# A fused transformer block on one core: unscaled probabilities with inverse sums on the value product, and a front that keeps batch 0 on chip and splits the weights

## What is computed

```python
xn = _layernorm(x, axis=-1)
x = x + attention(xn, w_q, w_kv, w_proj, b_proj) + ffn(xn, ...)

# attention: 16 heads of 32, one key and one value head for all of them, rotary positions
attn = jnp.einsum('bnih,bjh->bnij', q, k)
attn = jnp.where(causal, -jnp.finfo(attn.dtype).max, attn)
attn = jax.nn.softmax(attn, axis=-1)
out = jnp.einsum('bnij,bjd->bind', attn, v)
out = out.reshape(B, S, N_HEADS * HEAD_DIM) @ w_proj.T + b_proj

# ffn: gate logits pick 2 of 4 groups, then 8 of 32 experts for each token;
# every expert works on a latent x @ fc1_w.T of 256; a shared part runs for all tokens
shared = relu2(x @ shared_up_w.T) @ shared_down_w.T
return shared + (sum over picked experts, weighted) @ fc2_w.T
```

## Time and profile before

| | us |
|---|---|
| median of 3 runs | 1771.65 (1771.54 to 1773.84) |
| the profiled execution, span | 1784.5 |
| PE busy | 1640.6 (92%) |
| DVE busy | 1202.6 (67%) |
| ACT busy | 1073.5 (60%) |
| POOL busy | 822.7 (46%) |
| front, about | 100 |
| middle, batch 0, mask to mask | 161.5 |
| middle, each of batches 1 to 6 | 119.1 to 122.0 |

### The profile page before, as it was taken

How to read it: one execution, slowest core, us unless ns; L and a number is a source line. 1 busy time by engine, 2 the same in 40 slices (tenths; PEclk the granted TensorE clock), 3 DMA queues, 4 the chain that set the end, 5 groups by cost and what they waited for, 6 DMA issues and landing times.

```text
span 1784.5 us, 40620 instructions
## 1 busy us (share of the span) xinstructions
PE 1640.6 (92%) x10811; PEld 1385.8 (78%) x10811; DVE 1202.6 (67%) x3666; ACT 1073.5 (60%) x2799; POOL 822.7 (46%) x669
## 2 busy tenths in 40 slices
PE   5836779999999999999999999899999999999999
PEld 5835557777777777777777777689999999999987
DVE  7857876877777867767778678355555555555567
ACT  2324545775675756757757667466666666666652
POOL 0032101442443424434424345177777777777760
PEclk9967889999999999999999999999999999999999
DMA  7983242443434434435434344489999999998894
GB/s 283 372 279 88 55 71 79 137 128 101 157 115 144 126 99 131 135 103 153 137 104 133 102 146 122 135 154 184 186 185 195 194 177 197 210 176 159 139 251 187
DMA packets 193666, 277.91 MB, mean 156 GB/s; under 512 B 37464, under 2 KB 133855, under 8 KB 190884
## 3 DMA queue, kind: packets, MB, share of 16 engines
q0 software_dynamic: 60352, 92.59, 23.9%
q1 hardware_dynamic: 78148, 117.20, 23.0%
q10 hardware_dynamic: 54944, 65.52, 12.5%
HBM read 123.93 MB, written 131.76 MB: 143 GB/s over the span
## 4 chain that ended last, share of the span: by engine, by line
PE 63%; DVE 12%; issue 8%; ACT 4%; DMA 3%; POOL 2%; DVEq 1%; SPq 0%; another core or an unknown queue 0%; ACTq 0%; POOLq 0%
PE e_psH L1644 12%; PE e_psY L1655 11%; PE m_psT L1250 6%; PE m_psU L64 4%; DVE m_sc L1047 4%; PE m_psU L66 4%; PE m_psS L1233 4%; PE m_psU L65 4%; PE m_psO L1274 4%; PE e_psX L1629 3%; PE m_psY L66 3%; PE m_psY L64 3%; PE m_psY L65 3%; POOL sums L1609 2%; ACT m_sc L899 2%
## 5 line engine op out<-in xcount | busy, mean ns | idle before, releaser
L1609 POOL DMA_INDIRECT sums<-e_y,e_where x287 | 445.3, 1551 | 156.5 <-issue 94.4
L823 POOL DMA_INDIRECT slot_rows<-m_row,slots x256 | 268.6, 1049 | 501.1 <-ACT m_sc L899 457.2
L899 ACT ACTIVATE m_sc<-m_sc,m_low 128x512 f32<-128x512 f32 (+3 forms) x512 | 283.7, 557 | 173.9 <-DVE m_low L1047 150.8
L1644 PE MATMUL e_psH<-e_xt,e_w_of 128*128 128x128 f32 x2296 | 303.6, 275 | 3.2 <-ACT e_xt L1504 3.2
L1047 DVE CUSTOM_DVE_ANT_0 m_sc<-m_psS,cst 128x512 f32<-128x512 f32 (+3 forms) x512 | 230.0, 485 | 107.0 <-PE m_psS L1233 104.8
L1655 PE MATMUL e_psY<-e_w,e_ht 128*128 x1148 | 295.7, 380 | 2.3 <-ACT e_ht L1515 2.1
L1644 PEld LDWEIGHTS e_psH<-e_xt,e_w_of 128*128 128x128 f32 x2296 | 279.0, 192 | 3.7 <-ACT e_xt L1504 3.5
L1510 ACT ACTIVATE e_w_of<-e_w 128x512 f32 x287 | 180.9, 630 | 120.9 <-issue 119.0
L1250 PE MATMUL m_psT<-cst,m_sc 128*128 128x128 f32 x1280 | 204.1, 280 | 10.5 <-ACT m_pt L910 9.4
L1655 PEld LDWEIGHTS e_psY<-e_w,e_ht 128*128 128x128 f32 x1148 | 196.2, 191 | 18.0 <-issue 3.2
L1233 PE MATMUL m_psS<-m_ks,m_qs 96*128 96x256 f32 (+2 forms) x512 | 156.6, 371 | 57.4 <-DVE m_low L1047 39.8
(11 more groups left out here) (204 smaller groups left out, 3166.1 us busy)
## 6 DMA issues: line engine op xcount, KB each, us to landing
e_row<-slot_rows ACTq DMA_DIRECT2D x287, 144.5 KB
m_qs<-m_qhi SPq DMA_DIRECT2D x256, 64.0 KB
e_w<-in_w SPq DMA_DIRECT2D x256, 64.0 KB
f_xt<-in_x SPq DMA_DIRECT2D x8, 1024.0 KB, 9.5
xnt_hi<-f_hi SPq DMA_DIRECT2D x8, 1024.0 KB, 4.5
xnt_lo<-f_lo SPq DMA_DIRECT2D x8, 1024.0 KB, 8.1
m_qs<-m_qlo SPq DMA_DIRECT2D x128, 64.0 KB
m_res<-in_x SPq DMA_DIRECT2D x8, 1024.0 KB
```

Of the source, the lines that this page charges most:

```text
L823: pool.indirect_dma_start(out=xs, out_offset=bass.IndirectOffsetOnAxis(ap=slots_sb[:, g, k:k + 1], axis=0), in_=row[g % 2][:, :], in_offse ...
L899: nc.scalar.activation(cols, cols, ACT.Exp, bias=low[:, h % 2, i:i + 1], scale=-1.0, accum_out=total[:, h % 2, i:i + 1]).then_inc(exp_done, 1)
L1609: pool.indirect_dma_start(out=both_sums, out_offset=bass.IndirectOffsetOnAxis(ap=where[u % NY][:, 0:1], axis=0), in_=y[u % NY][:, :], in_o ...
L1644: mm = pe.matmul(psH[u % 2][:, k * P:(k + 1) * P], w1_of[u % 2][:, c * INTER + k * P:c * INTER + (k + 1) * P], xt[u % 2][:, c * P:(c + 1) ...
```

## The change

It has two parts.

**Attention.** The probabilities stay unscaled. VectorE only makes the reciprocals (`invert`), kept for four heads in `inv`. For each chunk c of four heads, VectorE broadcasts them to 128 x 512 in `ot` (`spread`, slots 4, 8, 12, 16, between the mask of row 2 and the squares), TensorE transposes that with four transposes into m_psU (`inverses`, slots 5, 9, 13, 17, ahead of the scores of rows 1 and 0), ScalarE copies it to `ot` (`copy_inverses`, between the exponentials of rows 2 and 1), and VectorE multiplies the product with the values by it (`normalise`, behind the reciprocal). `keep` is gone; in slot 17 `highs` rounds four chunks of `ot`. The transposes wait for the exponentials, the mask no longer for `scaled`. In batch 0 the broadcast of chunk 1, in slot 8, waits for `tagged_saved`.

**Front.** The groups come in order 1 to 7, then 0, and batch 0's halves are made in `xh` and `xlo` and stay there. The 21 pieces of the weights are loaded during the front (1, 5, 3, 3, 3, 3, 3 and 0 with the eight groups), rounded on ScalarE behind each group's work, and subtracted on GpSimd. The middle issues the bias and then stacks.

```diff
@@ -107,8 +107,8 @@
...
-        hi = [sb(f"f_hi{u}", [P, KC, S], F32R) for u in range(R)]
-        lo = [sb(f"f_lo{u}", [P, KC, S], F32R) for u in range(R)]
+        hi, lo = [sb("f_hi", [P, KC, S], F32R), xh], [sb("f_lo", [P, KC, S], F32R), xlo]
+        xn = sb("f_xn", [P, TB, D])
@@ -155,18 +167,26 @@
             def load(i, u):
...
-                sp.dma_start(xt[u][:, :, :], x[bass.ds(i * R * S + u * S, S), :].rearrange("(i p) d -> p i d", p=P)
+                sp.dma_start(xt[u][:, :, :], x[bass.ds(group(i, u) * S, S), :].rearrange("(i p) d -> p i d", p=P)
...
+            def load_pieces(i, u):
+                for k in range(*PIECES_OF[i * R + u]):
+                    if k >= UNDER_WAY:
+                        sp.wait_ge(piece_in[k % UNDER_WAY], 16 * (k // UNDER_WAY))
+                    sp.dma_start(part(1, PIECES[k]), part(0, PIECES[k])).then_inc(piece_in[k % UNDER_WAY], 16)
             def store_halves(i, u):
+                if group(i, u) == 0:
+                    return
...
-                    sp.dma_start(to[bass.ds(i * R + u, 1)].rearrange("a p c s -> (a p) c s"),
+                    sp.dma_start(to[bass.ds(group(i, u), 1)].rearrange("a p c s -> (a p) c s"),
...
-            in_a_row(((0, load), (2, store_halves)), B, R)
+            in_a_row(((0, load), (0, load_pieces), (2, store_halves)), B, R)
...
-                sp.wait_ge(xnt_saved[u], stored(B // R - 1, u))
+                sp.wait_ge(xnt_saved[u], stored(B // R - 1 - u, u))
@@ -201,11 +221,22 @@
...
-                act.dma_start(rows[bass.ds(i * R * S + u * S, S), 0:LAT].rearrange("(i p) l -> p i l", p=P),
+                act.dma_start(rows[bass.ds(group(i, u) * S, S), 0:LAT].rearrange("(i p) l -> p i l", p=P),
...
-            in_a_row(((0, root), (1, high), (2, latent)), B, R)
+            def high_pieces(i, u):
+                for k in range(*PIECES_OF[i * R + u]):
+                    act.wait_ge(piece_in[k % UNDER_WAY], 16 * (k // UNDER_WAY + 1))
+                    nc.scalar.activation(part(2, PIECES[k]), part(1, PIECES[k]), ACT.Copy).then_inc(piece_hi_made, 1)
+            in_a_row(((0, root), (1, high), (2, latent), (1, high_pieces)), B, R)
...
+        @block.gpsimd
+        def _(pool):
+            for k, piece in enumerate(PIECES):
+                pool.wait_ge(piece_hi_made, k + 1)
+                nc.gpsimd.tensor_tensor(part(3, piece), part(1, piece), part(2, piece).bitcast(F32), ALU.subtract).then_inc(piece_lo_made, 1)
...
         def _(pe):
@@ -299,21 +330,21 @@
...
-PIECE_AT = {p: k + 1 for k, p in enumerate(PIECES)}
-SPLIT_FIRST, SPLIT_NEXT, SPLIT_BEFORE, SPLIT_A_SLOT = 4, 8, 10, 2
+PIECES_A_GROUP = (1, 5, 3, 3, 3, 3, 3, 0)
+PIECES_OF = [(sum(PIECES_A_GROUP[:n]), sum(PIECES_A_GROUP[:n + 1])) for n in range(B)]
...
@@ -339,39 +370,19 @@
...
-    def load_inputs(self, sp, halves):
+    def load_bias(self, sp):
...
-        for piece in PIECES[:2]:
-            self.load_piece(sp, piece)
-        for to, src in halves:
-            sp.dma_start(to[:, :, :].bitcast(F32), src[0]).then_inc(self.x_in, 16)
-        for piece in PIECES[2:]:
-            self.load_piece(sp, piece)
     def save_weights(self, sp):
@@ -635,9 +636,14 @@
...
+INV_AT = {HC * _c + HC + 1: _c for _c in range(KC)}
...
-for _s in range(NH):
-    U_ORDER.append(f"up{_s}")
+for _s in range(NSLOT):
+    if _s in INV_AT:
+        U_ORDER.append(f"inv{INV_AT[_s]}")
+    if _s < NH:
+        U_ORDER.append(f"up{_s}")
@@ -882,13 +888,10 @@
...
-            routing.high_parts(act, 0, SPLIT_FIRST)
...
-            routing.high_parts(act, SPLIT_FIRST, SPLIT_NEXT)
...
-            routing.high_parts(act, SPLIT_NEXT, SPLIT_BEFORE)
             def batch(b, first):
                 def exps(h, i):
@@ -911,19 +914,18 @@
...
-                def keep(c):
-                    act.wait_ge(pv_done, at(b, KC, c + 1))
+                def copy_inverses(c):
+                    act.wait_ge(u_done, at(b, NU, U_AT[f"inv{c}"] + 1))
+                    nc.scalar.activation(ot[:, c, :], psU[:, :], ACT.Copy).then_inc(inv_copied, 1)
+                def highs():
+                    act.wait_ge(pv_done, at(b, KC, KC))
...
-                    if first and c == 1:
-                        act.wait_ge(routing.tagged_saved, 16)
-                    if c == KC - 1:
-                        for k in range(c):
-                            nc.scalar.activation(oh[:, k, :], ot[:, k, :], ACT.Copy).then_inc(oh_made, 1)
-                        act.sem_inc(o_out, 1)
-                        nc.scalar.activation(oh[:, c, :], psO[:, :], ACT.Copy).then_inc(oh_made, 1)
-                        return
-                    nc.scalar.activation(ot[:, c, :], psO[:, :], ACT.Copy).then_inc(o_out, 1)
+                    for k in range(KC):
+                        act.wait_ge(o_out, at(b, KC, k + 1))
+                        nc.scalar.activation(oh[:, k, :], ot[:, k, :], ACT.Copy).then_inc(oh_made, 1)
                 def shared(s):
@@ -937,16 +939,21 @@
...
-                        for i in ROWS:
-                            exps(s, i)
+                        exps(s, ROWS[0])
+                        exps(s, ROWS[1])
+                    if s in INV_AT:
+                        copy_inverses(INV_AT[s])
+                    if s < NH:
+                        exps(s, ROWS[2])
+                        exps(s, ROWS[3])
                     if s == 2 and not first:
...
-                    if s > HC and s % HC == 1:
-                        keep(s // HC - 1)
+                    if s == NSLOT - 1:
+                        highs()
@@ -1041,21 +1045,28 @@
...
-                        dve.wait_ge(scaled, at(b, NH, h - 1))
...
-                def scale(h):
+                def invert(h):
...
-                    nc.vector.reciprocal(inv[:, h % 2, :], total[:, h % 2, :]).then_inc(inv_made, 1)
-                    dve.wait_ge(inv_made, at(b, NH, h + 1))
-                    for i in range(TB):
-                        cols = sc[:, h % 2, SPC[i]:SPC[i] + (i + 1) * P]
-                        last = nc.vector.tensor_scalar(cols, cols, inv[:, h % 2, i:i + 1], None, ALU.mult)
-                    last.then_inc(scaled, 1)
+                    nc.vector.reciprocal(inv[:, h // HC % 2, :, h % HC], total[:, h % 2, :]).then_inc(inv_made, 1)
+                def spread(c):
+                    dve.wait_ge(inv_made, at(b, NH, HC * (c + 1)))
+                    if first and c == 1:
+                        dve.wait_ge(routing.tagged_saved, 16)
+                    nc.vector.tensor_copy(ot[:, c, :].rearrange("p (k d) -> p k d", d=HD),
+                                          inv[:, c % 2, :, :].rearrange("p i n -> p (i n)").unsqueeze(2).broadcast_to([P, TB * HC, HD])
+                                          ).then_inc(inv_spread, 1)
+                def normalise(c):
+                    dve.wait_ge(pv_done, at(b, KC, c + 1))
+                    dve.wait_ge(inv_copied, at(b, KC, c + 1))
+                    nc.vector.tensor_tensor(ot[:, c, :], psO[:, :], ot[:, c, :], ALU.mult).then_inc(o_out, 1)
                 def shared(s):
@@ -1071,6 +1082,8 @@
...
+                    if s + 1 in INV_AT:
+                        spread(INV_AT[s + 1])
@@ -1086,9 +1099,11 @@
...
-                        scale(s)
+                        invert(s)
...
+                    if s in INV_AT:
+                        normalise(INV_AT[s])
@@ -1117,7 +1132,7 @@
...
-                    nc.vector.tensor_tensor(ol[:, c, :], psO[:, :] if c == KC - 1 else ot[:, c, :], oh[:, c, :].bitcast(F32),
+                    nc.vector.tensor_tensor(ol[:, c, :], ot[:, c, :], oh[:, c, :].bitcast(F32),
@@ -1192,7 +1207,6 @@
...
-            pe.wait_ge(routing.x_in, 32)
@@ -1249,6 +1259,14 @@
...
+                def inverses(c):
+                    bank_free(b, f"inv{c}")
+                    pe.wait_ge(inv_spread, at(b, KC, c + 1))
+                    for i in range(TB):
+                        mm = pe.transpose(psU[:, i * P:(i + 1) * P], ot[:, c, i * P:(i + 1) * P], ident)
+                    mm.then_inc(u_done, 1)
                 def values(c, key_tiles):
@@ -1285,6 +1303,8 @@
...
+                    if s in INV_AT:
+                        inverses(INV_AT[s])
...
```

75 lines of the change are left out of this document (27 added, 48 removed).

## The result

The changed kernel takes 1784.98 us (median of 4 runs, 1784.24 to 1787.01), the kernel before 1772.74 beside it. The ratio is 1.0069, with a 95% interval of 1.0055 to 1.0083: 12.2 us slower. The forecast was 1789.8, in a range of 1764 to 1802, with a chance of 0.72 on slower.

What follows compares the result with a forecast made beforehand. TensorE carried 63% of the chain, VectorE led the front, and scaling lay beside the slot's loop. 14 − 16.9 + 9.3 + 11.7 = +18.1 on the 1784.5 us span: 1802.6, or 1789.8 in the median's terms; range 1764 to 1802.

Steps and rivals of the forecast that it cites:

- The front: Stretch before the middle: GpSimd's subtractions hold up VectorE's operations, plus up to 1 us of transfers; +14 us (0 to 22).
- The 2.3 us a burst: Front: VectorE's loss per burst of three GpSimd subtractions, taken between 0 and 3.8 us, for 5.7 bursts.
- Rival (1): Front not slowed by GpSimd, as a one-input shuffle row suggests: front +1, total +5.1, 1776.8 us; chance .19.
- Transfers: Front: DMA moves 4.25 MB a group against 3.5, on engines with a share of 1.02; 0 to +1 us.
- Rival (5): Front worse: DMA takes 10.8 us a group against 9.46, +9 and collisions, 1800 us; chance .10.
- The start: Start of the middle: halves on chip and pieces split, so VectorE becomes the limit and the mask comes earlier; −16.9 us.
- Batch 0: Slots 0 to 4 gain 5.4; slot 8's broadcast stalls 12.4 for the table's save, then 2.3 for TensorE's clock; +9.3 us.
- Rival (2): Batch 0: the save is out by 222, the stall is 2 and the clock stays; −12.7, 1777.1 us; chance .11.
- +0: Rest of batch 0, beyond slots 0 to 4 and the loss in slots 7 and 8: no change.
- Settled batches: Batches 1 to 7: transposes 1.27 and broadcasts 1.5 added, scaling's removal −1.1; +1.7 us a batch, +11.7 in all.
- Rival (3): Settled batches: scaling is really on the loop, −4 us a batch, −28 in all, 1750 us; chance .09.
- 120.8, not 119.1: Sign to look for: length in us of a settled batch after the change, against before.

Runs made afterwards that it cites:

- experiment 4: Whole change with GpSimd's front subtractions held back until VectorE has copied the group's logits, later ones until the statistics are done; 1777.84 us.
- the second profile: Kernel before, unchanged, profiled again; span 1769.7 us, measured time 1771.53 us.
- the first: Profile of the kernel before that the forecast was worked from, later found an outlier; span 1784.5 us.
- experiment 5: Whole change with SyncE issuing the routing table's save ahead of the third stack of queries instead of behind it; 1767.89 us.
- experiment 2: Kernel before with only the attention part (unscaled probabilities with inverse sums), front and weight pieces as before; 1794.95 us.
- 3: Kernel before with only the new front, scaling of the probabilities as before; 1763.16 us.
- 8: Whole change with subtractions held back, pieces spread 1, 8, 3, 1, 0, 0, 2, 6, save ahead of third stack, broadcast behind masks; 1753.37 us.
- 9: Whole change with TensorE turning only one of the four tiles of each chunk's inverses; 1778.95 us.

## Why the prediction held, step by step

The forecast was +18.1 us and +12.2 was measured. Four of the five steps were put too dear, by 0.5 to 2.1 us each, and the gain of the start 0.2 too large; the mechanism of each is the one that the runs show.

**The front, +12.4 for +14.** Right in its mechanism and nearly in size, if the bias at 111 to 116 us in the other runs with this front is kept in mind. The 2.3 us a burst were chosen between 0 and 3.8; the two full collisions cost 4.88 − 1.92 = 2.96 each, the third, at 44 to 50, 0.95 + 2.18 = 3.1, and two bursts met only small operations (0.99 for 0.17 at the most). Five to six bursts at 2.3 was a mean over an uneven lot, and that it came out is in part luck. Rival (1), no slowing of one-input operations, is excluded by the 4.88. Its evidence, the STREAM_SHUFFLE of the earlier trace rows, was from another kind of operation: statistics and shuffles pass a subtraction, normalise and copies don't. The Trainium skill (SBUF — State Buffer, "🔬 SBUF: two separate sides") says that copies and tensor-scalar operations in a two-port mode take the shared ports and block whole; by the 4.88 and 2.61 the trace agrees. The statistics, which it does not name among them, keep their 2.47 beside two subtractions (experiment 4).

**Transfers, +1 at most.** Right for this kernel, which has no wait for tokens, though nothing was set against it. Rival (5) had the transfers as a bound with +9; experiment 4 shows that 4.8 us of such a bound lay under GpSimd's. That the two do not add was luck: the forecast had not weighed it.

**The start, −16.7 for −16.9.** Right, by its steps: rotation straight after the group sums (128.91), which are the new limit, and the stack as soon as the high halves are there. Two differences cancel. From bias to mask the forecast had 26.6 us and it was 25.4: the group sums end 15.8 us after the bias for 16.3, and the scores come 8.5 us after them for 9.3, since the third transfer of the stack took 2.0 us to the scores and not 3.2. And before, the second profile has 42.1 for the 43.5 of the first.

**Batch 0, +7.2 for +9.3.** Right in its mechanism. The loss of slot 8 was 16.9 for 14.7: 14.3 of waiting for 12.4, and 2.6 for 2.3 behind it, with a clock at half speed for 12 us. The wait was mis-sized because the working read the save's end, 230 to 231, from the DMA share; it landed at 234.2 in that trace, 14.9 us after its issue. Rival (2), an early save, did not come, since the order on SyncE was unchanged; experiment 5 shows what it would have given. Slots 0 to 4 gave 5.1 for 5.4, but slot 4 needs both parts: 11.31 before, 11.62 with the attention part alone, 10.34 with the front alone, 9.35 with both. What the working had put at "+0" are slots 5, 11, 12 and 14, with −1.7, −1.0, −1.0 and −1.0. Slot 12 falls in every run without the scaling (8.32 for 9.34 in experiment 2) and not in 3: there other VectorE work stood behind the scaling too. Slot 11 does not belong with it: it is 10.20 in experiment 2, but 11.17 to 11.34 in 4, 8 and 9, which do not scale either, so its fall stays unexplained. In slot 5 the front part alone gives 1.0 (15.95).

**Settled batches, +1.45 for +1.7.** By the slots of the table, the broadcast was taken at 0.5 and cost 0.33, 0.36 and (net) 0.20, near the lower bound (the CAST of the earlier trace rows, 0.29): 0.9 for 1.5. The transposes were taken at 4 × 0.43 less 0.46 for waits that would take them up, 1.27, and cost 0.38 + 0.42 + 0.43 + 0.50 = 1.7: the price was right and nothing was taken up. The gain of slot 7 was 0.66, as worked out from the earlier trace rows, and that of all slots 1.15 for 1.1. So 0.9 + 1.7 − 1.15 = 1.5, with two errors of opposite sign, which is luck. (The upper bound of this part, 14 us for 0.61 a broadcast and no absorption, does not follow from its terms: they give 3 × 0.61 + 1.73 − 1.1 = 2.5 a batch, 17 in all.) Rival (3), the scaling on the loop, is excluded by experiments 2 and 3.

That the rows came from an unusual execution cost little. The working went by differences inside slots, and slots 4 to 10 of batch 2 are the same in both profiles to 0.1 us. A forecast for a batch of "120.8, not 119.1" was 0.8 too high, 0.6 of it for that reason.

## What to carry to other kernels

An engine's busy time is worth removing only where its operation is what the next one waits for: a settled batch lost 15.9 us of VectorE's work here and grew by 1.5, since 0.4 us on the busiest engine and 0.34 us ahead of a mask were put in its place, every fourth head. An added wait is paid by everything that stands behind it in the engine's order, so it goes behind the work that others wait for, and what it waits for goes ahead in its own queue; two such moves of a few lines gave 17 us each, in part the same ones. And when work is moved under an engine that seems to have room, look both at the ports that it shares and at the transfers, for the one will hide the other until it is mended.

## What the runs showed of the hardware

- A GpSimd two-input operation of 128x512 float32 (1.27 us) holds up VectorE's TENSOR_SCALAR and COPY from SBUF to SBUF, until it ends: four normalise operations, 1.92 us together when alone, took 4.88 beside three, four copies of 32 columns 2.61 instead of 0.43. Statistics, and subtractions with one input from PSUM, kept their 2.47 and 2.48.
- A broadcast COPY from 16 values to 128x512 took 0.42 us, with 0.34 to the next instruction: less than a two-input operation of the size (0.68).
- The save of the table, 528 KB in pieces of 132 bytes, took 13.9 us from issue to landing with a stack and a load of 1 MB around it, 14.9 in the first profile of before, and 12.5 in experiment 5, where the next stack was issued 11 us after it.
- TensorE stopped near 209 us in the changed kernel; its clock was granted at 0.66 in 210 to 214, and at 0.50 from there to 226, though it worked again from 222 on.
